# A decoder layer in one program: gathers moved behind low halves, transposes ahead of the first query, and another order at the end of cross attention

## The chip, the cores and the metric

The kernel runs on one core of a Trainium2 chip. The metric is the device time of one execution in microseconds (us). Five engines take part, each with its own instruction stream: TensorE (PE) multiplies, VectorE (DVE), ScalarE (ACT) and GpSimd (POOL) work elementwise, and SyncE (SP) issues DMAs. They wait for each other through semaphores that the kernel places by hand.

## The reference, cut to what matters

The input `x` is 32 sequences of 64 tokens of width 512, so 2048 rows. Three blocks follow one another, each added to its input and normalised:

```python
x = layernorm(x + self_attention(x))     # 32 heads of 128, 8 key heads; keys are 16 cache blocks of 32 rows, k_cache[block_idx], and sequence 0's own 64
x = layernorm(x + cross_attention(x, ctx))   # 32 heads, 8 key heads, keys and values from ctx (same shape as x)
z = x @ W.T + b                          # 512 to 512
m = (x @ A) @ B * p                      # 8 experts of rank 16, summed
gamma = minimum(0.5 * norm(z) / (norm(m) + eps), 1)
x = layernorm(x + z + gamma * m)
```

In self attention all 2048 rows see the same 576 keys. In cross attention each sequence sees its own 64.

## The kernel before, in words

Every float32 product is made of three products of a high and a low half: `a_hi b_hi + a_lo b_hi + a_hi b_lo`. ACT writes the high half (a rounded copy), DVE or POOL the low half (the difference). So each operand passes PE's bank, ACT, then DVE or POOL, before PE may use it.

**Phase one, self attention (`GROUPS` = 64 groups k).** A group is two heads for one half of the rows. Each has 8 score tiles `i` of 128 rows by 576 keys: PE `score(i)`, DVE `maximum(i)`, ACT `exponent(i)`, DVE `turn(i)` (a transpose in blocks), ACT `turned_hi(i)` (the high half, `pth`), POOL `low(i)` (the low half, `ptl`). The tile `8(k+1)` and up are made while group k is in `values(k)`, which waits for `low(8k+7)`. Then `project(k, t)`, t = 0 to 3, applies `wo`. `k = 4g + c`: four groups share one key head g. At c = 0, 1, 2 a small task prepares the next head's new keys, the turned keys and the new values. POOL also issues the indirect DMAs: `gather_k(g+2)` at c = 3 and `gather_v(g+1)` at c = 1, four each, from the cache blocks that `block_idx` names; ACT's `values_hi` and POOL's `values_low` split what was gathered.

**The start.** PE runs `query(0, 0)`, `turn_keys(0)`, and on through the first scores, with `query(1, 1)` behind `score(6)`. `query(0,0)` needs x tiles 0 to 3 and the first weight, in both halves. DVE's list of low halves and maxima is written by hand: `FIRST` are the loads (x tiles, `wq`, `wk`, `wv`).

**Phase two, cross attention (`STEPS` = 64 steps n).** A step is one head of 16 sequences: PE runs `score2(n)`, `values2(n-1)`, two blocks of the query of a later step, `project2(n-1, 0)` and `(n-1, 1)`, and keys and values of the next key head (`key2`, and `value_rows2` for odd heads). DVE sums and turns the scores, subtracts the maxima, inverts the sums and turns back. The layer norm of earlier tiles is spread over steps: `NORM_STEPS` and `NORM3_STEPS` say at which steps DVE and ACT normalise a pair of tiles. PSUM banks are handed round in an order that `bank_order` computes from the PE order, and `LAST_BANKS` names a few.

**The end.** In steps 60 to 63 the first eight tiles of x3 (the input of the last block) are turned by `turn_acc`, and split into `yTh`, `yTl`. `low_rank(q)` multiplies four tiles with A into `u`, `low_rank_out(tt)` with B, `linear(tt)` with W. Behind the last step each engine closes its semaphores and waits for all others (`"two"`), then phase three runs over 16 tiles `tt`: PE turns tile `tt+6`, does `linear(tt)` and `low_rank_out(tt)`; ACT takes norms (`norm_z`, `norm_m`, `norm_root`, `scaled_m`), DVE does `z_out` and `mix`, POOL `add_z` and `add_m`. `low_rank(q)` comes at `tt % 4 == 3`.

The lines that the rows below name: L1865 is `products` (all three-term sums), L1858 `turn_blocks`, L1937 `score`, L1957 `values`, L774 the indirect DMA in `gather`, L799 `low` on POOL, L534 and L571 the low halves of weights and the rotation, L954 ACT's high half of the gathered values, L529 ACT's high half of a load, L1457 `statistics`, L1690 the sum of scores, L1680 the swap of halves, L1412 `query_lo`, L1358 the low half of x tiles turned, L1540 `low_rank_lo`.

## Time and profile before

| | |
|---|---|
| time, median of 3 runs | 2743.34 us (2742.24 to 2744.5) |
| profiled execution, time | 2743.87 us |
| profiled execution, span | 2742.1 us |
| PE busy | 2684.1 us, 98% |
| DVE, POOL, ACT busy | 74%, 59%, 56% |
| mean granted clock of PE | 0.994 |

Phase one runs to about 1640 us, cross attention to about 2665, the last block to the end. How to read it: the busy share of an engine is an average over the span. "Idle before" in a timeline row is the time for which the engine stood still ahead of that instruction, and the arrow names the instruction that released it. The granted clock is 1.00 for 2.4 GHz and 0.50 for 1.2 GHz.

### The profile page before, as it was taken

The numbers are of one execution on the slowest core, as the hardware profiler recorded it, in microseconds if no ns is written. First come the engines' busy times: TensorE is split into PE (matmuls) and PEld (weight loads), VectorE is DVE, ScalarE is ACT, GpSimd is POOL, SyncE is SP. The second block draws the span as 40 slices with busy tenths as digits, with TensorE's granted clock in tenths as the row PEclk, the third lists the DMA queues.
The fourth block names the chain that finished last, engine by engine and source line by source line (L and its number), as shares of the span: only waits on it lengthen the run. The fifth ranks groups of instructions, "written<-read, shape, count | busy, mean of one in ns | idle before, by whom it ended". The sixth has DMA issues, their size and how long they took to land.

```text
span 2742.1 us, 64050 instructions
## 1 busy us (share of the span) xinstructions
PE 2684.1 (98%) x26496; PEld 2374.8 (87%) x26496; DVE 2022.1 (74%) x4005; ACT 1537.9 (56%) x3207; POOL 1621.1 (59%) x1379
## 2 busy tenths in 40 slices
PE   7999999999999999999999999999999999999997
PEld 6889888889899999999998988888888888888876
DVE  6676667667677777667777668887778878777887
ACT  5566566656666665666665645554445455444445
POOL 6887887788777666676666763232324433333235
PEclk9999999999999999999999999999999999999998
DMA  6233223323325313322331331111112111111111
GB/s 177 77 93 99 86 80 103 94 70 104 107 61 168 92 48 88 84 72 72 84 87 52 83 98 43 35 54 39 45 41 59 51 43 40 50 35 43 32 32 62
DMA packets 91483, 197.70 MB, mean 72 GB/s; under 512 B 20664, under 2 KB 21304, under 8 KB 89144
## 3 DMA queue, kind: packets, MB, share of 16 engines
q1 hardware_dynamic: 71480, 154.80, 20.2%
q10 hardware_dynamic: 17664, 34.61, 3.8%
q8 instruction: 209, 3.42, 0.5%
q0 software_dynamic: 2048, 4.20, 0.5%
q14 instruction: 82, 0.67, 0.1%
HBM read 176.78 MB, written 16.78 MB: 71 GB/s over the span
## 4 chain that ended last, share of the span: by engine, by line
PE 84%; POOL 7%; DVE 5%; issue 2%; ACT 1%; DMA 0%; DVEq 0%; ACTq 0%
PE bank L1865 29%; PE big L1865 28%; PE bank L1957 14%; PE big L1937 12%; POOL ptl L799 3%; POOL gathered L774 2%; PE big L1957 2%; POOL wqTl L534 1%; ACT pth L981 0%; DVE xol L1514 0%; DVE P L1690 0%; POOL wkvTl L534 0%; PE big L1858 0%; POOL oTl L804 0%; DVE nmx L1417 0%
## 5 line engine op out<-in xcount | busy, mean ns | idle before, releaser
L799 POOL TENSOR_TENSOR ptl<-P,pth 128x576 fp32r<-128x576 f32 x512 | 727.5, 1438 | 291.1 <-ACT pth L981 290.6
L972 ACT ACTIVATE P<-big,nmx 128x576 f32<-128x576 f32 x512 | 378.4, 739 | 345.8 <-DVE nmx L1417 313.5
L1423 DVE STREAM_TRANSPOSE P<-P 128x576 f32<-128x576 f32 x512 | 395.2, 772 | 152.6 <-ACT P L972 147.2
L1957 PE MATMUL bank<-pth,v 32*128 32x256 f32 x4608 | 426.9, 282 | 11.0 <-POOL ptl L799 8.2
L1417 DVE TENSOR_REDUCE nmx<-big 128x1 f32<-128x576 f32 x512 | 384.8, 753 | 71.3 <-PE big L1937 58.2
L1957 PE MATMUL big<-pth,v 32*128 32x256 f32 x4608 | 427.4, 282 | 0.5 <-issue 0.4
L1957 PEld LDWEIGHTS bank<-pth,v 32*128 32x128 f32 x4608 | 364.6, 188 | 22.3 <-POOL ptl L799 11.9
L1957 PEld LDWEIGHTS big<-pth,v 32*128 32x128 f32 x4608 | 369.4, 188 | 1.0 <-issue 1.0
L981 ACT ACTIVATE pth<-P 128x576 fp32r<-128x576 f32 x512 | 340.6, 678 | 39.7 <-DVE P L1423 39.4
L880 POOL TENSOR_TENSOR P<-P,sm 128x512 f32<-128x512 f32 x64 | 67.3, 1051 | 487.3 <-DVE sm L1719 487.3
L1957 PE MATMUL big<-ptl,v 32*128 32x256 f32 x2304 | 336.4, 279 | 0.0
L1957 PE MATMUL bank<-ptl,v 32*128 32x256 f32 x2304 | 331.0, 279 | 0.0
L1957 PEld LDWEIGHTS big<-ptl,v 32*128 32x128 f32 x2304 | 231.3, 188 | 0.0
L1937 PE MATMUL big<-kTh,qTh 128*128 128x288 f32 x1024 | 224.9, 301 | 6.6 <-ACT P L972 5.8
L804 POOL TENSOR_TENSOR oTl<-rall,oTh 128x256 fp32r<-128x256 f32 x256 | 183.5, 740 | 80.3 <-ACT oTh L987 80.3
L1957 PEld LDWEIGHTS bank<-ptl,v 32*128 32x128 f32 x2304 | 226.1, 188 | 0.0
L1937 PE MATMUL big<-kTl,qTh 128*128 128x288 f32 x1024 | 220.1, 296 | 0.0
L1937 PE MATMUL big<-kTh,qTl 128*128 128x288 f32 x1024 | 219.0, 295 | 0.0
L1937 PEld LDWEIGHTS big<-kTh,qTh 128*128 128x128 f32 x1024 | 180.5, 189 | 41.5 <-ACT P L972 6.1
L987 ACT ACTIVATE oTh<-rall 128x256 fp32r<-128x256 f32 x256 | 93.4, 412 | 187.4 <-DVE rall L1439 187.4
L1439 DVE TENSOR_TENSOR rall<-bank,rall 128x256 f32<-128x256 f32 x128 | 48.3, 419 | 200.8 <-PE big L1957 200.8
L534 POOL TENSOR_TENSOR wqTl<-raw,wqTh 128x512 fp32r<-128x512 f32 x126 | 162.1, 1298 | 7.2 <-ACT wqTh L529 6.9
(283 smaller groups left out, 8008.5 us busy)
## 6 DMA issues: line engine op xcount, KB each, us to landing
rall<-kept_r ACTq DMA_DIRECT2D x64, 512.0 KB
raw<-in_wo SPq DMA_DIRECT2D x64, 256.0 KB
raw<-in_xWq SPq DMA_DIRECT2D x64, 256.0 KB
raw<-in_xWo SPq DMA_DIRECT2D x64, 256.0 KB
raw<-in_wq SPq DMA_DIRECT2D x62, 256.0 KB
v<-kept_v SPq DMA_DIRECT2D x24, 448.0 KB
v<-kept_v SPq DMA_DIRECT2D x68, 128.0 KB, 3.0
raw<-in_xWkv SPq DMA_DIRECT2D x32, 256.0 KB
```

What stands on the lines that cost most here:

```text
L534: engine.tensor_tensor(lo, split_source(kind, n), f(hi), ALU.subtract).then_inc(signal((kind, n)), 1)
L799: pool.tensor_tensor(third_columns(ptl, i), blocks_of(i), f(third_columns(pth, i)), ALU.subtract).then_inc(p_low(i), 1)
L804: pool.tensor_tensor(out_quarter(ol[:, :, :], a), rall_quarter(a), f(out_quarter(oh[:, :, :], a)), ALU.subtract).then_inc(o_low((k, a)), 1)
L880: pool.tensor_tensor(pv, pv, sm2[:, :].unsqueeze(2).to_broadcast([128, 16, 32]), ALU.mult).then_inc(p_norm((2, n)), 1)
L972: act.activation(P[:, i % PSLOTS, :].rearrange("p (k n) -> p k n", k=2), ps_s[i % 2][:, :, 0:HALF], ACT.Exp, bias=nmx[:, i % 8:i % 8 + 1], ...
L981: act.activation(third_columns(pth, i), blocks_of(i), ACT.Copy).then_inc(p_hi(i), 1)
L987: act.activation(out_quarter(oh[:, :, :], a), rall_quarter(a), ACT.Copy).then_inc(o_hi((k, a)), 1)
L1417: dve.tensor_reduce(nmx[:, i % 8:i % 8 + 1], ps_s[i % 2][:, :, 0:HALF], AX.XY, ALU.max, negate=True).then_inc(max_done(i), 1)
L1423: dve.transpose(P[:, i % PSLOTS, :], P[:, i % PSLOTS, :]).then_inc(p_turned(i), 1)
L1865: t = pe.matmul(dst, a, b, start=first and i == 0, stop=final and end)
L1937: m = pe.matmul(ps_s[i % 2][:, h, 0:HALF], l, r[:, HALF * h:HALF * h + HALF], start=j == 0, stop=j == 2)
L1957: m = pe.matmul(ps_o[a][:, 0:256], v[r, s, l, :], p[r, lo:hi + 1:hi - lo, block_of(b), :, :], start=first, stop=final)
```

## The change: what it does

- **Gathers.** In groups `4g+1` POOL issues `gather_v(g+1)` behind `low(8(k+1)+6)` and `+7` and no longer behind `+5`.
- **Start.** PE makes 40 transposes of the identity into a score bank ahead of `query(0,0)`. The transposes' result isn't read. DVE takes three of the low halves of `FIRST` earlier (6, 7 ahead of the rotation, 8 ahead of the first maximum), `maximum(8)` ahead of `turn(7)` and `query_lo(1,1)` behind it; ACT takes `query_hi(1,1)` behind `exponent(7)`; PE takes `query(1,1)` ahead of `score(6)`.
- **Norms.** The last of the four norms in each half of cross attention moves from step 9 to 12 and from 41 to 44.
- **End.** The steps 62 and 63 are written out on PE, ACT and DVE in a new order. Tiles of x3 at steps 60 and 61 go to the banks of the values. `linear(0)` and `linear(1)` have banks of their own; `linear(2)`, `linear(3)`, `low_rank_out(0)` and `(1)` stand ahead of the last projection. `low_rank` 1, 2, 3 come at `tt` 1, 7, 11 (before: ahead of the last projection, 7, 11 on PE, 3, 7, 11 on ACT and DVE), and the odd ones go to another buffer (`low_rank_at`). ACT's norms and DVE's mixing of tiles 0 and 1, and POOL's `add_z` of both, stand ahead of the wait `"two"`.
- A few SBUF buffers stand in another order.

```diff
-NORM_STEPS = (5, 6, 7, 9)
-NORM3_STEPS = (37, 38, 39, 41)
+LOW_RANK_TILES = (1, 7, 11)
+NORM_STEPS = (5, 6, 7, 12)
+NORM3_STEPS = (37, 38, 39, 44)
...
-LAST_BANKS = [(("w", STEPS - 1, 0), 3), (("w", STEPS - 1, 1), 1)]
+LAST_BANKS = [(("u", 0), 0), (("w", STEPS - 3, 0), 1), (("w", STEPS - 3, 1), 3), (("x3", 4), 2), (("x3", 5), 0),
+              (("z", 0), 1), (("x3", 6), 3), (("x3", 7), 2), (("z", 1), 0), (("w", STEPS - 2, 0), 1),
+              (("w", STEPS - 2, 1), 3), (("w", STEPS - 1, 0), 0), (("w", STEPS - 1, 1), 1)]
...
+        def low_rank_at(q):
+            return (uTh, uTl) if q % 2 == 0 else (flat(q2h[:, 0]), flat(q2l[:, 0]))
...
-                if 0 <= g < G - 1 and c == 1:
-                    gather_v(g + 1)
...
+                if 0 <= g < G - 1 and c == 1:
+                    gather_v(g + 1)
...
+            add_z(0)
+            add_z(1)
...
-                if q >= 1:
-                    gate.wait_ge(ff_done, ("m", 4 * q - 1))
+                if q == 1:
+                    gate.wait_ge(s_done, (2, STEPS - 1, 1))
+                elif q >= 2:
+                    gate.wait_ge(ff_done, ("m", 4 * q - 5))
...
+            query_hi(1, 1)
+            exponent(8)
             turned_hi(7)
             keep_sums(0)
-            exponent(8)
             exponent(9)
             turned_hi(8)
             turned_hi(9)
-            query_hi(1, 1)
...
+            n = STEPS - 2
+            low_scores(n)
+            out2_hi(n - 1)
+            for a in blocks_at(n // 4, n % 4):
+                weight2(*a)
+            low_rank_hi(0)
+            exponential(n)
+            for tt in early_x3(n):
+                tile_high("x3", tt)
+            probability_hi(n)
+            n = STEPS - 1
+            low_scores(n)
+            out2_hi(n - 1)
+            for tt in early_x3(n):
+                tile_high("x3", tt)
+            exponential(n)
+            probability_hi(n)
+            out2_hi(n)
...
+            norm_z(0)
+            norm_m(0)
+            norm_root(0)
+            norm_z(1)
+            norm_m(1)
+            scaled_m(0)
+            norm_root(1)
+            scaled_m(1)
+            for s in (*of_pe, *of_dve, *of_pool, in_bob, in_pcol, *in_raw):
+                gate.wait_ge(s, "two")
...
+            weight_low(*FIRST[6])
+            weight_low(*FIRST[7])
             rotate(dve, gate, prep, 0)
             query_lo(0, 0)
             key_lo(0)
             new_key_lo(0, ps_o[1])
-            weight_low(*FIRST[6])
-            weight_low(*FIRST[7])
+            weight_low(*FIRST[8])
...
+            maximum(8)
             turn(7)
+            query_lo(1, 1)
             invert_sums(0)
-            maximum(8)
             maximum(9)
             turn(8)
             turn(9)
-            query_lo(1, 1)
...
+            n = STEPS - 2
+            sum_scores(n)
+            out2_lo(n - 1)
+            turn_scores(n)
+            maxima(n)
+            low_rank_lo(0)
+            half_sums(n)
+            add_out2(n - 1, 0)
+            invert_sums2(n)
+            turn_back(n)
+            add_out2(n - 1, 1)
+            for tt in early_x3(n):
+                tile_low("x3", tt)
+            z_out(0)
+            n = STEPS - 1
+            sum_scores(n)
+            out2_lo(n - 1)
+            tile_low("x3", early_x3(n)[0])
+            turn_scores(n)
+            maxima(n)
+            tile_low("x3", early_x3(n)[1])
+            half_sums(n)
+            invert_sums2(n)
+            z_out(1)
+            turn_back(n)
+            add_out2(n - 1, 0)
+            add_out2(n - 1, 1)
+            statistics(pairs2(GG - 1, 0), 2)
+            statistics(pairs2(GG - 1, 1), 2)
+            out2_lo(n)
...
+            add_out2(STEPS - 1, 0)
+            for tt in range(2):
+                for step in range(4):
+                    mix(tt, step + 1)
+                z_out(tt + 2)
+            add_out2(STEPS - 1, 1)
+            for s in (*of_dve, acc_done, ln):
+                s.close("two")
+            for s in (*of_pe, *of_act, *of_pool, in_bob, in_pcol, *in_raw):
+                gate.wait_ge(s, "two")
...
+            gate.wait_ge(pool_init, "ident")
+            for i in range(40):
+                pe.transpose(ps_s[0][:, 0, 0:128], ident[:, :], ident[:, :])
...
-            score(6)
             query(1, 1)
-            for i in range(7, 12):
+            for i in range(6, 12):
...
+            n = STEPS - 2
+            score2(n)
+            values2(n - 1)
+            low_rank(0)
+            project2(n - 1, 0)
+            project2(n - 1, 1)
+            for tt in early_x3(n):
+                turn_acc("x3", tt)
+            linear(0)
+            n = STEPS - 1
+            score2(n)
+            for tt in early_x3(n):
+                turn_acc("x3", tt)
+            values2(n - 1)
+            linear(1)
+            project2(n - 1, 0)
+            project2(n - 1, 1)
+            low_rank(1)
+            linear(2)
+            values2(n)
+            linear(3)
+            project2(n, 0)
+            wait_over(0)
+            low_rank_out(0)
+            wait_over(1)
+            low_rank_out(1)
+            project2(n, 1)
+            ring[0] = 0
...
-                if tt % 4 == 3 and 2 <= tt // 4 + 1 < 4:
-                    low_rank(tt // 4 + 1)
+                if tt in LOW_RANK_TILES[1:]:
+                    low_rank(LOW_RANK_TILES.index(tt) + 1)
                 if tt >= NT - 2:
                     low_rank_out(tt)
-                if tt >= 2:
+                if tt >= 4:
                     linear(tt)
-                if tt < NT - 2:
+                if 2 <= tt < NT - 2:
```

## Rows read from the trace of the kernel before

**Rows 1.** The page, busy time of each engine
```profile
PE 2684.1 (98%) x26496; PEld 2374.8 (87%) x26496; DVE 2022.1 (74%) x4005; ACT 1537.9 (56%) x3207; POOL 1621.1 (59%) x1379
```

**Rows 2.** Waits of PE, whole span: us in total, times, longest
```profile
PE bank L1957 <- POOL ptl L799: 8.2, 7, 2.9
```

**Rows 3.** Timeline of PE, starts of values: start, us, operation, idle before
```profile
74.28 0.38 PE L1957 MATMUL bank<-pth,v 32*128 32x256 f32 x2
...
103.04 0.58 PE L1957 MATMUL bank<-pth,v 32*128 32x256 f32 x2 [2.88 <-POOL ptl L799]
...
179.28 0.38 PE L1957 MATMUL bank<-pth,v 32*128 32x256 f32 x2
...
204.93 0.38 PE L1957 MATMUL bank<-pth,v 32*128 32x256 f32 x2 [0.91 <-POOL ptl L799]
...
757.04 0.38 PE L1957 MATMUL bank<-pth,v 32*128 32x256 f32 x2
...
781.24 0.38 PE L1957 MATMUL bank<-pth,v 32*128 32x256 f32 x2
```

**Rows 4.** Windows: PE, PEld, DVE, ACT, POOL busy; clock, DMA share, GB/s
```profile
103.00:106.00 3.00, 2.96 (x56) 2.96 (x60) 1.15 (x2) 2.63 (x6) 3.00 (x3) 0.50 0.03 5
```

**Rows 5.** Timeline of POOL in group 5, gathers and low halves
```profile
194.82 0.98 POOL L774 DMA_INDIRECT gathered<-in_v_cache,idx  x1
...
202.09 5.58 POOL L799 TENSOR_TENSOR ptl<-P,pth 128x576 fp32r<-128x576 f32 x4
```

**Rows 6.** Windows of the cross-attention steps 9, 10 and 11
```profile
1781.85:1796.26 14.41, 14.41 (x83) 12.24 (x81) 12.60 (x29) 7.81 (x15) 6.26 (x6) 1.00 0.24 73
1796.26:1811.53 15.27, 14.84 (x82) 12.07 (x81) 12.54 (x34) 8.16 (x14) 3.49 (x3) 1.00 0.12 35
1811.53:1826.97 15.44, 14.54 (x82) 12.24 (x81) 12.93 (x31) 8.50 (x17) 7.47 (x7) 1.00 0.16 53
```

**Rows 7.** Timeline of DVE: the norm behind step 9, and score sums
```profile
1797.49 1.28 DVE L1457 BATCH_NORM_STATS2 stat<-xaccb 128x6 f32<-128x512 f32 x2
...
1800.65 1.41 DVE L1690 TENSOR_TENSOR P<-big,P 64x512 f32<-64x512 f32 x2
...
1845.57 1.41 DVE L1690 TENSOR_TENSOR P<-big,P 64x512 f32<-64x512 f32 x2 [2.29 <-ACT P L1202]
```

**Rows 8.** Timeline of PE at the start
```profile
8.95 0.76 PE L1865 MATMUL bank<-xTh,wqTh 128*128 128x512 f32 x1 [8.95 <-issue]
...
14.95 0.63 PE L1858 MATMUL big<-ident,gathered 128*128 128x128 f32 x4 [0.74 <-DVE gathered L571]
...
27.01 0.50 PE L1865 MATMUL bank<-xTh,wqTh 128*128 128x512 f32 x1 [1.06 <-DVE xTl L534]
...
46.66 0.58 PE L1957 MATMUL bank<-pth,v 32*128 32x256 f32 x2 [1.49 <-DVE qTl L1412]
```

**Rows 9.** Timeline of ACT behind the start
```profile
53.50 0.63 ACT L529 ACTIVATE wqTh<-raw 128x512 fp32r<-128x512 f32 x1 [3.90 <-DMA raw<-in_wq]
```

**Rows 10.** Windows, from step 61 to PE's last instruction
```profile
2600.00:2727.50 127.50, 119.69 (x576) 96.58 (x574) 104.52 (x264) 66.05 (x158) 58.11 (x46) 0.97 0.11 38
```

**Rows 11.** Timelines of PE, DVE and POOL at the end
```profile
2679.31 0.51 PE L1865 MATMUL big<-wkvTh,uTh 128*128 128x512 f32 x1 [1.99 <-DVE uTl L1540]
...
2673.96 0.60 PE L1858 MATMUL big<-ident,xaccb 128*128 128x128 f32 x4
...
2671.87 0.69 DVE L1358 TENSOR_TENSOR yTl<-big,yTh 128x512 fp32r<-128x512 f32 x1 [2.06 <-ACT yTh L920]
...
2630.02 2.19 DVE L1680 TENSOR_TENSOR mxo<-mx 32x16 f32<-32x16 f32 x4
...
2629.24 2.54 POOL L534 TENSOR_TENSOR xTl<-raw,xTh 128x512 fp32r<-128x512 f32 x2 [1.27 <-ACT xTh L529]
```

**Rows 12.** The chain of waits at the start; timeline of ACT in group 5
```profile
7.44 4.99 DMA gathered<-in_k_cache,idx
...
217.88 0.62 ACT L954 ACTIVATE gathered<-gathered 128x512 fp32r<-128x512 f32 x1
```

More of the change, by code:

```diff
@@ L1192, in scalar_program, with low_scores @@
             value2_hi(0, 2)
-            for n in range(STEPS):
-                g, s = n // 4, n % 4
-                work = blocks_at(g, s)
-                last = n == STEPS - 1
+            rows2 = flat(P2[:, :, :])
+            def low_scores(n):
                 for par in range(2):
@@ L1280, in scaled_m, with shift_tile @@
                     ff_hi(("gm", tt)), 1)
+            for s in (*of_act, root):
+                s.close("two")
+            norm_z(0)
[8 more added lines that the diff above has]
+                gate.wait_ge(s, "two")
+            def shift_tile(tt):
+                gate.wait_ge(ln, ("shift", 3, tt))
+                act.activation(xa(tt), xa(tt), ACT.Identity, bias=mv[:, tt, 0:1], scale=rstd[:, tt:tt + 1]).then_inc(
+                    ff_hi(("norm", tt)), 1)
             for tt in range(NT):
@@ L1321, in put @@
                 turn += 1
-            for n in range(STEPS):
+            for n in range(STEPS - 2):
                 g, s = n // 4, n % 4
@@ L1336, in bank_order @@
                     put(("w", n - 1, 1))
-                if n < STEPS - 2:
-                    for tt in early_x3(n):
-                        put(("x3", tt))
                 if n == 0:
```

239 lines of the change are left out of this document (103 added, 136 removed).

## The prediction

> **What bounds the kernel now.** I read the page's engine table first: TensorE (PE) is busy 98% of a span of 2742.1 us, VectorE (DVE) 74%, the others less [rows 1]. So PE's instruction stream sets the end, and an edit is worth only what it takes from PE's idle time, from PE's time at the lower clock, or from the tail behind PE's last matmul. Second, the waits of PE over the whole span: the largest entry is PE waiting in `values` for the low half of the probabilities from GpSimd (POOL), 8.2 us in seven waits, the longest 2.9 [rows 2]. Third, the timeline of PE at the starts of `values(k)`: the reader should compare intervals. Two neighbours with nothing extra lie 24.20 apart (757.04 to 781.24); 179.28 to 204.93, where keys are also turned, is 25.65 and ends in an idle 0.91 on POOL; 74.28 to 103.04 is 28.76 and ends in an idle 2.88 [rows 3]. Behind that last wait PE runs 3 us at a granted clock of 0.50, 1.2 GHz of 2.4, after an idle stretch [rows 4]. The other losses of PE sit at two steps of cross attention, in the first 47 us, and behind 2600 us; each is read below.
>
> **Gathers behind low halves.** In group k = 4g+1 POOL issues four indirect DMAs for the values of the next key head between the low half of tile 5 and those of tiles 6 and 7 of the next row. They occupy it from 194.82 to about 199.5, then come two weight low halves, and only at 202.09 the run of `low`s whose second one `values(6)` waits for at 204.93 [rows 3, 5]. Four issues at 0.95 plus three pauses of 0.3 are 4.7 us, and PE waits 0.9: with the gathers behind the two `low`s these end some 4 us before PE asks, and the whole stall goes. It occurs six times at 0.9 (8.2 less the 2.9) = 5.4. The first time costs more: 28.76 against 25.65 less 0.91 is 4.0, and three microseconds at half clock give back 1.5. Sum 10.9. At most 11.4 (if a restart of PE costs 0.1 more each time), at least the idle time alone, 8.2. What is now late: the gathers move past `low(8(k+1)+6)` and `+7` and stand ahead of `low(8(k+2))`, `+1`, which are delayed by no more than before since POOL's work ahead of them is the same. ACT's exponents of the next row wait for those two; they are asked for about 6 us later, by my reading of the same timeline. The similar gather of keys in groups 4g+3 stays.
>
> **Norms from steps 9 and 41 to 12 and 44.** A step of cross attention with an even head takes 14.41; the two behind step 9's norm take 15.27 and 15.44 [rows 6]: 0.86 + 1.03 = 1.9, and the same again at 41, so 3.8. The block holds DVE from 1797.49 to 1800.65, 3.16 us [rows 7]. Steps 12 and 44 have an odd head and more matmuls (`value_rows2`). There DVE sits idle 2.29 before its next score sum [rows 7], so the block makes that sum 0.87 late, where before a block of 3.16 cost a step 0.86 and 1.03 with no such idle time ahead of it. I take the 0.87 as hidden; if all of it reached PE, twice, 2.0 of 3.8 is left.
>
> **The start.** `query(0,0)` begins at 8.95, when DVE's low half of the inputs is there, and ends at 14.21; the turn of the keys then waits 0.74 for DVE's rotation, which hangs on the gather of keys [rows 8]. Forty transposes ahead of it end before 8.95 (four take 0.60 at most [rows 11], forty 6.0, from about 1.5), so they cost nothing, and a faster first query gains nothing, because its end is not what is late. The DVE order counts: x tile 5's low half moves ahead of the first maximum, so the wait of 1.06 at 27.01 goes; `query_lo(1,1)` moves up on DVE and ACT, so the wait of 1.49 at 46.66 goes [rows 8]: 2.6. The two low halves moved ahead of the rotation fit into the time in which DVE waits for the gather (the chain of waits has that DMA to 12.43 [rows 12]). `score(6)` goes behind `query(1,1)`, hidden as DVE reaches its maximum only later. The interval 46.66 to 74.28 is 27.62 [rows 3, 8], 2.0 over the 25.65 of a later one, which I lay to the lower clock behind idle PE; I take a third of it back, 0.6. Sum 3.2. The next bound is ACT, which waits 3.90 for a weight load at 53.50 and holds the exponent that `score(13)` needs [rows 9]; that chain also moves, but by about 2.6. Bounds: -1 (the scores before `values(0)` now leave PE idle in more pieces and may run at the lower clock) and +5.
>
> **The end.** From 2600 to PE's end at 2727.5 PE is busy 119.69 of 127.5 and its clock is 0.97 [rows 10]: 7.8 idle and 3.8 of clock, 11.6 to be had at most. The new order puts tiles of x3 into the banks of the values, starts `linear(0)` in step 62 instead of 63, does `linear(2)`, `linear(3)` and two `low_rank_out` ahead of the last projection, computes the second low-rank tile into its own buffer, and puts ACT's and DVE's norms of tiles 0 and 1 ahead of the wait common to all engines. The work is the same; it fills the holes of steps 62 and 63. By my walk through those steps with the durations of before PE reaches the last projection at about the same time as now but with 6.8 us more done (two times 2.73 and 0.68). This can't be kept whole: DVE gets to the low half of tile 8 at 2671.87 now, after waiting 2.06 [rows 11]; in the new order it has the norms of tiles 0 and 1, two z sums and the low half of u ahead of it, and I put it at 2671.2. PE needs it for its turn of tile 10, at 2673.96 now [rows 11]: 2.7 gained. The wait of 1.99 for u at 2679.31 [rows 11] goes (u has been ready for 8 us), and with it a fall of the clock like the one of rows 4, 1.5. Sum 6.2; bounds 2.0 (only the wait for u) and 11.6. From there DVE has 3.6 us of work for a tile of 3.9 on PE, estimated from the same timeline, so it follows.
>
> One row speaks for less. At 2630.02 four copies of 32 partitions take DVE 2.19 us, ending with POOL's weight low halves that began at 2629.24 [rows 11]. The Trainium skill (SBUF — State Buffer, "Who interferes with whom") says that a DVE instruction with two SBUF inputs and a GpSimd instruction that reads SBUF block each other for a whole instruction. By that rule the move of `add_z(0)`, `add_z(1)` to beside DVE's norms adds up to two such waits. The trace agrees, and at 1.3 a wait (the POOL row shows 2.54 for two) the end would give 3.6 instead of 6.2, which is within the bounds above.
>
> **Sum.** 10.9 + 3.8 + 3.2 + 6.2 = 24.1. The profiled execution took 2743.87, 1.8 more than its span and 0.5 more than the median 2743.34; 2743.9 - 24.1 = 2719.8, and on the scale of the median 2719.3. I say 2719.
>
> **Rivals.**
> A. DVE is the bound of the end: it is busy 104.5 of 127.5 there [rows 10], and taking PE's holes away only makes PE wait for DVE later. For it: DVE's share; against: it waits 2.06 at tile 8. The end gives nothing: 2725.5.
> B. The stall moves from POOL to ACT: the `low`s of the last two tiles are themselves held by ACT's high halves, so gathers out of the way gain nothing. Against it: the four `low`s from 202.09 run without a pause, 5.58 for four [rows 5], so POOL was the late one. 2743.4 - 13.2 = 2730.
> C. The transposes pay by themselves. The first query takes 5.3 for twelve matmuls, where the 576 matmuls and transposes behind 2600 take 0.21 each, 2.5 for twelve [rows 10]; if the query's end were what is late, 2.8 more would come. Against it: the 0.74 of rows 8. 2716.5. The Trainium skill (TensorE: Matmul & The Clock Gate, "What's actually happening") says the array starts throttled and activity releases it, by which the forty transposes would let the first query run at 2.4 GHz; the rows at 8.95 and 27.01 (0.76 and 0.50 for a first matmul) agree that the start is slow.
> D. Slower: the gather lands too late for ACT. ACT's high half of the gathered values at 217.88 stands in front of its exponents [rows 12]. The gathers now end their issue near 205.5, and the one that the trace shows lands 5.0 after its issue began [rows 12], so 6 us are to spare. If landing took more than 11.5, ACT would wait, and PE behind it, seven times; from 15 us on it eats the 24 us of gain. At 20 it would be 60 - 24 lost: 2779.
> E. The changes hide behind each other and nothing moves: 2743.
>
> **Chances.** Forecast 0.75, A 0.11, B 0.05, C 0.03, D 0.03, E 0.03. The range takes in A and most of the bounds: lows of the four parts together would give 2731, highs 2711; 2712 to 2729 should hold 8 times in 10. About 0.2% (5.5 us) can be told from no change: faster by more 0.94, within 0.03, slower 0.03.
>
> **What would show it.** In the trace after: no wait of PE on POOL in `values` at k = 4g+2, and the intervals of `values` there near 24.7; steps 10, 11, 42, 43 at 14.41, and 13, 45 at 17.3; `values(0)` near 44; turns of x3 tiles with no wait on u; PE's clock above 0.97 behind 2600. Wrong, if PE waits for ACT's exponents behind the gathered values, if steps 13 or 45 grow, or if DVE is busy without a pause from 2640 on while PE waits.

## The result, and the profile after

| | before | after |
|---|---|---|
| time, median of 4 runs | 2742.79 us (2740.95 to 2744.5) | 2727.61 us (2726.09 to 2728.54) |
| profiled execution, time and span | 2743.87, 2742.1 | 2728.54, 2726.7 |
| mean granted clock of PE | 0.994 | 0.992 |

The ratio is 0.9941, with a 95% interval of 0.9929 to 0.9953: the kernel is 15.2 us faster by the medians. I had said 2719, 24 us faster, with a range of 2712 to 2729. So the direction and the range held, the range by 1.4 us, and 9 of the 24 us did not come. The page of the changed kernel, part 1, stands against [rows 1]: PE has hardly more to do (40 transposes), and its idle time is less.

```profile
PE 2687.8 (99%) x26536; PEld 2381.6 (87%) x26536; DVE 2022.2 (74%) x4005; ACT 1539.0 (56%) x3207; POOL 1621.5 (59%) x1379
```

In the rows of the changed kernel the lines have other numbers: L1934 is `products`, L1927 `turn_blocks`, L2006 `score`, L2026 `values`, L780 the indirect DMA, L805 `low` on POOL, L535 and L540 the halves of a load, L570 to L577 the rotation, L962 ACT's high half of the gathered values, L1475 DVE's addition of a projection, L1388 the low half of x tiles turned, L1571 `low_rank_lo`, L1487 to L1501 a layer norm on DVE, L899 and L911 POOL's `add_z` and `add_m`.

The waits of PE in the changed kernel (us in total, times, longest). The entry of [rows 2], 8.2 us on POOL in `values`, is gone. Of the longest entries two were small or absent before, and both belong to parts that I had credited with a gain: the wait for DVE's `yTl` at the end, and that for the rotation (`gathered`) at the start.

```profile
PE big L1927 <- DVE yTl L1388: 4.6, 1, 4.6
...
PE big L1927 <- DVE gathered L577: 3.1, 1, 3.1
PE bank L2026 <- DVE xacc L1475: 2.0, 8, 0.6
```

Where the 15.3 us between the two traces lie is read from the starts of the same work in both, each from the timeline of PE. `score2(n)` is the first work of step n:

| start of | before | after | gained so far | gained in this stretch |
|---|---|---|---|---|
| `values(0)` | 46.66 | 46.75 | -0.1 | start: -0.1 |
| `values(1)` | 74.28 | 73.90 | 0.4 | 0.5 |
| `values(29)` | 781.24 | 772.03 | 9.2 | gathers: 8.8 |
| `values(63)` | 1602.33 | 1594.34 | 8.0 | -1.2 |
| `score2(60)` | 2593.97 | 2582.30 | 11.7 | norms: 3.7 |
| PE's last matmul | 2727.09 | 2711.75 | 15.3 | end: 3.7 |

The tail behind the last matmul is 15.0 us in both. The gathers gave 8.8 of 10.9, the norms 3.7 of 3.8, the end 3.7 of 6.2, the start nearly nothing of 3.2, and a place that I had not looked at took 1.2 back. This is one trace against one; the experiments below show which of these sizes return in other traces.

**Gathers.** Timelines of PE (the starts of `values(2)` and `values(6)`), POOL and ACT of the changed kernel; they answer to [rows 3, 5, 12].

```profile
98.84 0.38 PE L2026 MATMUL bank<-pth,v 32*128 32x256 f32 x2 [0.21 <-DVE xacc L1475]
...
198.74 0.39 PE L2026 MATMUL bank<-pth,v 32*128 32x256 f32 x2 [0.19 <-DVE xacc L1475]
...
193.88 1.43 POOL L805 TENSOR_TENSOR ptl<-P,pth 128x576 fp32r<-128x576 f32 x1 [0.79 <-ACT pth L989]
195.46 0.98 POOL L780 DMA_INDIRECT gathered<-in_v_cache,idx  x1 [0.15 <-issue]
...
200.22 2.83 POOL L805 TENSOR_TENSOR ptl<-P,pth 128x576 fp32r<-128x576 f32 x2
...
211.69 0.62 ACT L962 ACTIVATE gathered<-gathered 128x512 fp32r<-128x512 f32 x1
```

The low half that `values(6)` needs ends at 195.3, 3.4 us before the start, and the gathers follow it. PE no longer waits for POOL, but it waits 0.2 for DVE, which adds the last projection to the residual. So the interval went from 25.64 to 24.95, not to 24.74. ACT takes its high half of the gathered values at 211.69 with no idle time ahead of it.

**Norms.** Windows of steps 9 to 12 of cross attention (columns as in [rows 4]), against [rows 6].

```profile
1773.94:1788.36 14.42, 14.42 (x83) 12.25 (x81) 12.60 (x29) 7.83 (x15) 6.27 (x6) 1.00 0.26 74
1788.36:1802.77 14.41, 14.41 (x82) 12.24 (x81) 11.48 (x28) 7.33 (x14) 5.35 (x5) 1.00 0.12 36
1802.77:1817.18 14.41, 14.41 (x82) 12.24 (x81) 11.47 (x28) 6.81 (x13) 6.12 (x6) 1.00 0.22 56
1817.18:1834.48 17.30, 17.30 (x107) 15.13 (x105) 14.34 (x33) 9.08 (x16) 7.30 (x6) 1.00 0.15 46
```

Steps 10 and 11 are back at 14.41 with PE busy all the time, and so is step 12 at 17.30; steps 13 and 45 take 17.29 too. The block is free where it now stands.

### The profile page after: what moved, and what is told of

It reads as the page before. It is cut to its first block, busy times and chain, and to the rows that moved or that the text cites. A ratio compares the mean times of both kernels' runs of the same rounds, so it can differ in the third digit from the quotient of the medians.

```text
span 2726.7 us, 64132 instructions
## 1 busy us (share of the span) xinstructions
PE 2687.8 (99%) x26536; PEld 2381.6 (87%) x26536; DVE 2022.2 (74%) x4005; ACT 1539.0 (56%) x3207; POOL 1621.5 (59%) x1379
## 4 chain that ended last, share of the span: by engine, by line
PE 91%; DVE 4%; POOL 3%; ACT 1%; issue 1%; DMA 0%; SPq 0%; ACTq 0%; DVEq 0%
PE bank L1934 30%; PE big L1934 30%; PE bank L2026 14%; PE big L2006 14%; PE big L2026 2%; POOL ptl L805 1%; POOL gathered L780 1%; PE big L1927 0%; DVE P L1453 0%; DVE nmx L1447 0%; POOL wqTl L540 0%; DMA xacc<-in_xt 0%; ACT P L980 0%; DVE xacc L1475 0%; DVE xol L1544 0%
## 5 line engine op out<-in xcount | busy, mean ns | idle before, releaser
L805 POOL TENSOR_TENSOR ptl<-P,pth 128x576 fp32r<-128x576 f32 x512 | 728.2, 1437 | 295.3 <-ACT pth L989 294.7
L2026 PE MATMUL bank<-pth,v 32*128 32x256 f32 x4608 | 425.2, 281 | 2.9 <-DVE xacc L1475 2.0
L2026 PE MATMUL big<-pth,v 32*128 32x256 f32 x4608 | 425.3, 281 | 0.0
L2026 PEld LDWEIGHTS bank<-pth,v 32*128 32x128 f32 x4608 | 365.9, 187 | 14.1 <-issue 11.8
L2026 PEld LDWEIGHTS big<-pth,v 32*128 32x128 f32 x4608 | 367.4, 187 | 0.0
L2026 PE MATMUL big<-ptl,v 32*128 32x256 f32 x2304 | 334.9, 278 | 0.0
L2026 PE MATMUL bank<-ptl,v 32*128 32x256 f32 x2304 | 332.8, 278 | 0.0
L2006 PE MATMUL big<-kTh,qTh 128*128 128x288 f32 x1024 | 225.7, 302 | 5.2 <-ACT P L980 4.4
L2026 PEld LDWEIGHTS big<-ptl,v 32*128 32x128 f32 x2304 | 230.2, 187 | 0.2 <-issue 0.2
L2026 PEld LDWEIGHTS bank<-ptl,v 32*128 32x128 f32 x2304 | 228.1, 187 | 0.0
L2006 PE MATMUL big<-kTl,qTh 128*128 128x288 f32 x1024 | 220.9, 297 | 0.0
L2006 PE MATMUL big<-kTh,qTl 128*128 128x288 f32 x1024 | 219.6, 296 | 0.0
L2006 PEld LDWEIGHTS big<-kTh,qTh 128*128 128x128 f32 x1024 | 181.2, 189 | 40.1 <-ACT P L980 3.5
L2006 PEld LDWEIGHTS big<-kTh,qTl 128*128 128x128 f32 x1024 | 166.4, 190 | 0.0
```

The lines of the kernel that those rows point to most:

```text
L805: pool.tensor_tensor(third_columns(ptl, i), blocks_of(i), f(third_columns(pth, i)), ALU.subtract).then_inc(p_low(i), 1)
L2006: m = pe.matmul(ps_s[i % 2][:, h, 0:HALF], l, r[:, HALF * h:HALF * h + HALF], start=j == 0, stop=j == 2)
L2026: m = pe.matmul(ps_o[a][:, 0:256], v[r, s, l, :], p[r, lo:hi + 1:hi - lo, block_of(b), :, :], start=first, stop=final)
```

## The experiments

### The gathers alone

```diff
 # kernel before
-                if 0 <= g < G - 1 and c == 1:
-                    gather_v(g + 1)
...
                     low(8 * (k + 1) + 7)
+                if 0 <= g < G - 1 and c == 1:
+                    gather_v(g + 1)
```

> The kernel before with the gathers of values behind the two low halves and nothing else. Theory of the prediction (POOL issues four gathers while PE needs the low half): the idle of PE before the values of groups 4g+2 goes from 0.9 to what DVE leaves, about 0.2, the seven intervals from 25.65 to 24.95 and the first from 28.76 to about 25, its follower from 26.3 to 25.0: 9.3 us less at the start of values 29 (781.2 to 771.9), and 2734 us for the whole. Rival (the stall moves to ACT's high halves): the intervals stay at 25.6 and the time within 2 us of the kernel before. Rival (gathered values land too late): ACT waits ahead of the high half of the gathered values, and PE in groups 4g+3; slower than before.

Measured: 2733.23 us (6 runs, 2732.09 to 2733.96), ratio 0.9964 (0.9951 to 0.9976), 10 us faster. `values(29)` starts at 770.36, 10.9 earlier than before; but 2.5 of that is there at `values(1)` already (71.82 against 74.28), ahead of the first moved gather, in a start that has the same instructions. The part that the gathers can have made is 8.4. The six intervals at groups 4g+1 behind the first are 24.94 or 24.95, as in the changed kernel. The first is 25.65, where the changed kernel has 24.94 and 25 was expected: PE waited 0.46 more for the low half `oTl` on its way. Of the thirteen traces with the moved gathers seven have 24.94 there, one 25.09 and five 25.6 to 25.8, so this first interval is not a fixed number. ACT's wait did not come, so the theory stands and both rivals fall.

This run also showed that two traces of the same start can differ by 2.5 us, and that the interval from `values(62)` to `values(63)` was 23.02, as in the changed kernel, against 21.85 before: the 1.2 us lost there are not the work of any edit near it.

### The start, four ways, and the rotation ahead of two low halves

```diff
 # no_transposes and no_transposes_again: changed kernel
-            gate.wait_ge(pool_init, "ident")
-            for i in range(40):
-                pe.transpose(ps_s[0][:, 0, 0:128], ident[:, :], ident[:, :])
 # rotation_first: changed kernel
-            weight_low(*FIRST[6])
-            weight_low(*FIRST[7])
             rotate(dve, gate, prep, 0)
             query_lo(0, 0)
             key_lo(0)
             new_key_lo(0, ps_o[1])
+            weight_low(*FIRST[6])
+            weight_low(*FIRST[7])
 # start_old: changed kernel, but all of PE, DVE and ACT up to score 11 as before
 # start_old_transposes: start_old, with the 40 transposes
 # change_again: the changed kernel
```

> The changed kernel without the 40 transposes ahead of the first query. Theory 1 (the transposes only lengthen PE's idle behind the query, since the rotation of the keys is what is late, and the longer idle brings the clock down for longer): the first query runs at half clock again, 5.2 us instead of 2.8, the idle before the keys' turn is under 1 us instead of 3.1, the first score starts no later than 20.0 and values(0) starts 0 to 1.5 us earlier than 46.75. Theory 2 (the transposes bring what they are meant to and another edit eats it): values(0) starts 1 to 2.5 us later than 46.75, the whole takes 2729 to 2730.

> The changed kernel with DVE's low halves of the second weight and of x tile 4 back behind the rotation of the keys. Theory (these two wait for their loads, to 11.6 and 12.9, and hold the rotation back from 12.45 to 13.52): the rotation starts near 12.5, the keys' turn about 1 us earlier than 15.92, values(0) starts near 45.7 instead of 46.75, the whole takes about 1 us less. Rival (they fit into DVE's wait for the gather, and the later start in the changed kernel comes from loads of x that land later): the rotation starts at 13.5 again and values(0) at 46.7.

> The changed kernel itself, on the chip of the next three, so that the four make a square: with or without the 40 transposes, new or old order of the start. Expected 2726 to 2728.

> The changed kernel without the 40 transposes, once more and in more rounds. Theory (the transposes lengthen PE's idle and bring the clock down for longer): 1 to 2.5 us less than the changed kernel. Rival (the one look was luck, the transposes change nothing at the end of the start): within 0.7 us of it.

> The changed kernel with the whole start of before: no transposes, and the old order of PE, DVE and ACT up to score 11. The prediction gave the new start 3.2 us. Theory from the traces (the new start as a whole brings nothing or costs 1 us): this takes 0 to 1.5 us less than the changed kernel. Rival (the prediction's term): it takes 2 to 4 us more.

> The changed kernel with the old order of the start but with the 40 transposes. Theory (the rotation is not held back by low halves here, so the first query's 2.8 us again only lengthen the wait for it, to some 2 us): within 1 us of start_old, or up to 2 us more through the clock. Rival (the transposes pay when the order leaves them room): 1 to 2.5 us less than start_old.

Measured, with the start of `values(2)` in each trace (the first point behind the start; in the kernel before it would be at 99.2, that is 103.04 less the 3.8 that the gathers gave there):

| kernel | median us (runs) | lowest to highest | `values(2)` |
|---|---|---|---|
| change_again | 2725.17 (5) | 2723.71 to 2728.45 | 97.18 |
| no_transposes_again | 2727.24 (5) | 2725.52 to 2728.63 | 99.19 |
| start_old | 2727.08 (5) | 2724.77 to 2728.34 | 97.54 |
| start_old_transposes | 2727.51 (5) | 2724.25 to 2731.49 | 102.80 |
| no_transposes | 2725.95 (4) | 2724.98 to 2731.13 | 97.22 |
| rotation_first | 2728.43 (4) | 2725.23 to 2729.82 | 95.55 |

The first four ran on one chip. Their ratios to the kernel before are 0.9939, 0.9941, 0.9940 and 0.9940, each with an interval of about 3.6 us either way: the start as a whole, its transposes and its order are each worth nothing that these runs can tell. By the medians no_transposes_again is 2.1 us above change_again, which neither its theory nor its rival had, and start_old 1.9, just short of its rival's 2 to 4; the ranges overlap. The nine executions of the changed kernel (both sets) have a mean of 2726.6, the five of start_old 2726.7, and the difference is known to about 2 us; so a start worth 3.2 us is hardly left, one worth 1 us is. The traces say the same: `values(2)` comes at 99.2, 97.47 (gathers_only) and 97.54 with the old start, 98.1 on average, and at 96.74 to 100.74, 98.4 on average, in the five traces with the new one. The 2.5 us by which `values(0)` came earlier in no_transposes (44.28 against 46.75) were luck: the repetition gave 46.77 there, and the changed kernel's own repetition 45.25. The theory that the transposes cost 1 to 2.5 us fell in that repetition, and the prediction's 3.2 us fell as well.

rotation_first bore out its theory in the trace, where the rotation started at 11.55 and `values(0)` at 43.56, and not in the time: 2728.43 with a ratio of 0.9949, where 1 us less was expected. Its trace is of the fastest of its four executions; the others took 2728.07 to 2729.82.

What the traces do show is a mechanism on either side. Timelines of PE and DVE of the changed kernel, then PE of start_old:

```profile
9.85 0.47 PE L1934 MATMUL bank<-xTh,wqTh 128*128 128x512 f32 x1 [1.58 <-DVE xTl L540]
15.92 0.87 PE L1927 MATMUL big<-ident,gathered 128*128 128x128 f32 x4 [3.10 <-DVE gathered L577]
...
11.59 0.69 DVE L540 TENSOR_TENSOR wqTl<-xacc,wqTh 128x512 fp32r<-128x512 f32 x1 [0.62 <-ACT wqTh L535]
12.91 0.69 DVE L540 TENSOR_TENSOR xTl<-xacc,xTh 128x512 fp32r<-128x512 f32 x1 [0.63 <-ACT xTh L535]
13.52 0.75 DVE L570 TENSOR_TENSOR gathered<-gathered,turns 128x256 f32<-128x256 f32 x2
```

```profile
10.01 0.76 PE L1934 MATMUL bank<-xTh,wqTh 128*128 128x512 f32 x1 [10.01 <-DVE xTl L540]
14.26 0.60 PE L1927 MATMUL big<-ident,gathered 128*128 128x128 f32 x4
```

With the transposes the first query takes 2.97 us (from 9.85 to the turn's 15.92 less its wait), without them 4.25 in start_old and 5.26 before. So it is faster, as rival C said, but the keys' turn waits for DVE's rotation, and PE now stands still for 3.10 us. DVE in turn waits 0.62 and 0.63 for ACT's halves of loads that have just landed, and only then starts the rotation: the two low halves did not fit into its wait for the gather. In start_old the turn follows with no wait. When the gather lands differs from trace to trace, as the rotation shows where nothing else stands ahead of it; timelines of DVE in rotation_first and start_old_transposes:

```profile
11.55 0.76 DVE L570 TENSOR_TENSOR gathered<-gathered,turns 128x256 f32<-128x256 f32 x2 [1.28 <-DMA gathered<-in_k_cache,idx]
```

```profile
13.66 0.76 DVE L570 TENSOR_TENSOR gathered<-gathered,turns 128x256 f32<-128x256 f32 x2 [3.01 <-DMA gathered<-in_k_cache,idx]
```

Windows of 17 to 20 and 20 to 23 us of the changed kernel, then of start_old (columns as in [rows 4]):

```profile
17.00:20.00 3.00, 2.19 (x12) 2.08 (x11) 1.12 (x3) 1.20 (x4) 2.09 (x4) 0.50 0.14 44
20.00:23.00 3.00, 3.00 (x12) 3.00 (x13) 1.21 (x2) 1.48 (x4) 2.98 (x3) 0.50 0.18 49
```

```profile
17.00:20.00 3.00, 3.00 (x19) 2.74 (x20) 2.84 (x5) 2.23 (x5) 2.67 (x3) 1.00 0.18 45
20.00:23.00 3.00, 3.00 (x26) 2.77 (x25) 2.60 (x4) 2.81 (x6) 1.40 (x2) 1.00 0.00 0
```

start_old_transposes, where no low half stands ahead of the rotation, had the same wait in its trace, 3.54 us, and the same slow clock behind it, and the latest `values(2)` of all; but its gather landed last too, so this trace alone doesn't charge the transposes. The rival, that the transposes pay when the order leaves them room, has no support in its time either.

Behind the 3.10 us the clock is 0.50 for some 7 us, and what the faster query brings is spent. There is a second such place, ahead of `values(0)`. Windows of the changed kernel, then of start_old:

```profile
40.20:50.30 10.10, 8.61 (x82) 7.94 (x86) 6.48 (x11) 6.92 (x15) 5.50 (x5) 0.50 0.63 146
```

```profile
40.50:47.20 6.70, 5.87 (x60) 5.55 (x64) 4.30 (x6) 5.12 (x12) 0.92 (x2) 0.50 0.28 74
47.30:50.30 3.00, 3.00 (x109) 3.00 (x108) 0.00 (x0) 0.23 (x1) 3.00 (x3) 1.00 0.59 157
```

All fourteen traces have these places, and they give a rough split:

| | traces | PE's wait ahead of the turn | first score starts |
|---|---|---|---|
| 40 transposes, no filling behind the query | 7 | 1.83 to 3.98 | 16.69 to 20.40, mean 19.1 |
| no transposes | 5 | 0 to 1.42 | 16.93 to 18.07, mean 17.6 |

From the first score to `values(2)` the new order takes 78.7 to 81.1 us (eight traces without filling, 79.4 on average), the old order with the moved gathers 80.1 to 82.4 (three, 81.0), although the slow stretch ahead of `values(0)` lasts 10.2 us in five of those eight and 6.8 in every trace of the old order. So the new order of the scores is worth some 1.7 us, the transposes go with a first score some 1.5 us later, and the two cancel. The ranges overlap, and the low halves of x alone are ready up to 1.5 us apart from trace to trace (the first query started between 8.7 and 10.2), so these are sizes and not proofs.

### The clock: transposes in PE's waits

```diff
 # start_fill: rotation_first, and
             query(0, 0)
+            for i in range(10):
+                pe.transpose(ps_s[0][:, 0, 0:128], ident[:, :], ident[:, :])
             turn_keys(0)
...
             for i in range(6, 12):
+                if i >= 9:
+                    ps = out_place(1, None)
+                    for j in range({9: 9, 10: 6, 11: 3}[i]):
+                        pe.transpose(ps[:, 0:128], ident[:, :], ident[:, :])
                 score(i)
 # group_fill: changed kernel, in project(k, t)
                 ps = out_place(out_bank(k, t), (acc_done, (k, t)))
+                if k == GROUPS - 2 and t == 0:
+                    for i in range(9):
+                        pe.transpose(ps[:, 0:128], ident[:, :], ident[:, :])
 # end_fill: changed kernel, ahead of turn_acc("x3", 10)
+                if tt == 4:
+                    gate.wait_ge(ff_lo, ("z", 2))
+                    for i in range(24):
+                        pe.transpose(ps_z[0][:, 0:128], ident[:, :], ident[:, :])
```

> The changed kernel with 9 transposes of the identity into the output bank of the first projection of group 62, in PE's wait of 1.89 us there. Theory (behind this wait the clock falls, for 1.7 us before and for 5 us after the change, which took back 1.2 us of the gain): the interval from values 62 to values 63, 23.02 to 23.07 in four kernels and 21.84 in two, is 20.5 to 21.3. Rival (the interval is set by what the wait waits for, and its spread by chance of another kind): 21.8 to 23.1 again.

> The changed kernel with 24 transposes of the identity into an idle bank ahead of the turn of tile 10, where PE waited 4.64 us; their result is not read. Theory (the idle itself costs what DVE's lateness costs and nothing that PE does can change it, but the slow clock behind it is a second price): the wait shrinks to about 0.6 and the turn starts at the same distance from the last score sum, but the matmuls behind it start 0.23 apart and not 0.43, some 1.5 to 2 us less at PE's last matmul. Rival (the clock behind a wait is not the wait's doing): the matmuls behind the turn stay 0.43 apart for some 3 us, and the time is that of the changed kernel.

> rotation_first, and transposes of the identity in PE's waits of the start as well: 10 between the first query and the keys' turn, 9, 6 and 3 ahead of scores 9, 10 and 11. Theory (with the waits filled the clock stays at its high level from the first query on): first score near 16.7, the scores 1 to 8 1.5 to 2 us earlier, values(0) near 42.5 unless the loads of kept values hold it (it waited 1.36 for one at 44.28 without the transposes), and the interval to values(1) about 25 instead of 27.05; values(2) starts 2 to 4 us earlier than 95.55. Rival (the start is bound by DVE, ACT and loads): values(2) within 1 us of 95.55.

**group_fill**: 2725.02 us (4 runs, 2723.32 to 2727.71), within the spread of the changed kernel. The interval from `values(62)` to `values(63)` is 20.25, a little below the 20.5 to 21.3 expected. PE's timeline and a window of the changed kernel, then of group_fill:

```profile
1583.66 0.76 PE L1934 MATMUL bank<-woTh,oTh 128*128 128x512 f32 x1 [1.89 <-issue]
...
1585.00:1587.00 2.00, 2.00 (x7) 1.62 (x6) 0.13 (x1) 0.68 (x1) 2.00 (x2) 0.50 0.00 0
```

```profile
1583.49 1.15 PE L2036 MATMUL bank<-ident 128*128 128x128 f32 x9
1585.51 0.50 PE L1934 MATMUL bank<-woTh,oTh 128*128 128x512 f32 x1 [0.87 <-POOL oTl L810]
...
1583.00:1586.00 3.00, 2.13 (x16) 1.85 (x16) 2.10 (x3) 2.73 (x6) 3.00 (x5) 1.00 0.00 0
```

The wait is filed under "issue" in the one and under POOL's low half in the other, where the rest of it is 0.87; behind it the clock stays at 1.00. The fourteen traces have this interval in three groups: 21.6 to 21.9 in seven, 22.9 to 23.1 in five, and 20.25 and 20.30 in the two with the filling. The granted clock tells the groups apart: behind this wait it is 0.50 for 3.4 us in the seven, for 6.8 us in the five, and never in the two. Windows of the changed kernel (23.07), then of change_again (21.85):

```profile
1583.00:1589.70 6.70, 6.04 (x17) 5.10 (x18) 2.59 (x5) 3.35 (x7) 5.91 (x5) 0.50 0.15 39
```

```profile
1582.50:1585.70 3.20, 3.20 (x12) 2.82 (x11) 0.78 (x1) 1.23 (x3) 3.20 (x3) 0.50 0.00 0
1586.00:1589.70 3.70, 3.70 (x18) 3.04 (x17) 3.37 (x7) 1.52 (x3) 1.83 (x2) 1.00 0.24 71
```

The kernel before and the changed one, each profiled once, fell into different groups, and that is the 1.2 us of the table. change_again is the same code as the changed kernel. So this loss belongs to the profiled execution and not to the change.

**end_fill**: 2726.10 us (4 runs, 2725.25 to 2727.72), within the spread of the changed kernel; the trace resolves it. Timeline of PE and a window of the changed kernel, then of end_fill:

```profile
2660.72 1.12 PE L1927 MATMUL big<-ident,xaccb 128*128 128x128 f32 x4 [4.64 <-DVE yTl L1388]
...
2661.00:2664.00 3.00, 3.00 (x10) 2.52 (x10) 2.83 (x10) 1.84 (x6) 1.07 (x1) 0.50 0.02 5
```

```profile
2655.01 2.78 PE L2360 MATMUL big<-ident 128*128 128x128 f32 x24
2659.86 0.66 PE L1927 MATMUL big<-ident,xaccb 128*128 128x128 f32 x4 [2.06 <-DVE yTl L1388]
...
2661.00:2664.00 3.00, 3.00 (x15) 2.40 (x15) 2.26 (x7) 2.08 (x6) 1.95 (x2) 1.00 0.00 0
```

From the turn to PE's last matmul it is 49.1 us with the filling and 51.0 without: 1.9 us for the clock alone. The nine traces with the 4.64 us wait take 50.5 to 51.9 there. The transposes took 0.12 us each here, so 24 of them filled 2.8 us and not the 4 that I had meant, and 2.06 of waiting was left; that did not bring the clock down.

**start_fill**: 2723.90 us (4 runs, 2722.66 to 2724.59). Its ratio is 0.9931 (0.9915 to 0.9948), and it is 3.7 us below the changed kernel and 1.3 below change_again. The clock from 36 to 42 us is 1.00 where rotation_first had 0.56, `values(2)` starts at 94.49, 1.1 earlier than rotation_first and 2.3 to 6.3 earlier than in the five traces of the unchanged new start. The interval to `values(1)` is 27.05 again and not 25: the clock fell for 3.4 us just behind the start of `values(0)`, whose matmuls are 0.21 apart from 43.4 to 46.1 and 0.12 behind that. I had expected `values(2)` 2 to 4 us earlier than in rotation_first; 1.1 is hardly more than the 1 us of the rival. A part of the slow clock has another place than the waits that I filled, and rotation_first's trace was itself an early one.

### The norm of the last two tiles, later

```diff
 # changed kernel, ACT and DVE
-                if tt == 0:
+                if tt == 2:
                     square_root([NT - 2, NT - 1], 2)
...
-                if tt == 0:
+                if tt == 2:
                     normal3([NT - 2, NT - 1])
```

> The changed kernel with the layer norm of tiles 14 and 15 (DVE statistics and normalise, ACT's root) moved from tile step 0 to tile step 2 of the last block, behind the low half of tile 8. Theory (PE's 4.64 us wait ahead of the turn of tile 10 is DVE's and ACT's norm of tiles 14 and 15, 4.5 us, standing ahead of tile 8): the wait falls to under 1.5 us and the clock stays up, 3 to 5 us less, 2722.6 to 2724.6. Rival A of the prediction (DVE is the bound of the end, work moved behind one tile is paid at the next): the wait shows up again at the turns of tiles 11 to 13 and the whole gains less than 1.5 us.

Measured: 2723.91 us (4 runs, 2722.30 to 2725.08), 3.7 less than the changed kernel's 2727.61 and 1.3 less than change_again's 2725.17; the ratio is 0.9929 (0.9912 to 0.9945) against their 0.9941 and 0.9939. The time alone doesn't settle the size; the trace does. Timeline of DVE in the changed kernel: what stands between the last score work and tile 8's low half.

```profile
2654.80 1.29 DVE L1487 BATCH_NORM_STATS2 stat<-xaccb 128x6 f32<-128x512 f32 x2
...
2658.03 1.38 DVE L1501 TENSOR_SCALAR xaccb<-xaccb,mv,rstd 128x512 f32<-128x512 f32 x2
2659.33 0.74 DVE L1571 SCALAR_TENSOR_TENSOR xql<-bank,pcol,xqh 128x512 fp32r<-128x512 f32 x1
2659.99 1.49 DVE L1388 TENSOR_TENSOR yTl<-big,yTh 128x512 fp32r<-128x512 f32 x2
```

And with the norm later, DVE and then PE:

```profile
2655.45 0.75 DVE L1571 SCALAR_TENSOR_TENSOR xql<-bank,pcol,xqh 128x512 fp32r<-128x512 f32 x1 [0.78 <-PE big L1927]
2656.12 0.68 DVE L1388 TENSOR_TENSOR yTl<-big,yTh 128x512 fp32r<-128x512 f32 x1
2656.72 1.28 DVE L1487 BATCH_NORM_STATS2 stat<-xaccb 128x6 f32<-128x512 f32 x2
...
2656.86 0.66 PE L1927 MATMUL big<-ident,xaccb 128*128 128x128 f32 x4 [0.78 <-DVE yTl L1388]
2680.57 0.50 PE L1934 MATMUL bank<-wkvTh,uTh 128*128 128x512 f32 x1 [1.42 <-DVE uTl L1571]
```

The wait falls from 4.64 to 0.78, and PE's last matmul comes at 2708.30 instead of 2711.75, 3.45 earlier, with `score2(63)` at the same time in both (2625.30, 2625.27). 3.86 of wait and the slow clock went, 1.42 came back as a wait for u, and the rest is spent in small pieces. Rival A, DVE as the bound of the end, would have given the whole 3.86 back at the next tiles; of those 3.86 and the 1.9 of clock 2.3 were given back, less than half.

### All together

> start_fill, group_fill and last_norm_later in one. Theory (the three losses lie apart and add): 3 to 6 us from the start against the changed kernel, 2 from group 63, 3.4 from the end, so 2716 to 2719 us. Rival (they hide behind each other): 2722 to 2725.

The edits of start_fill, group_fill and last_norm_later in one kernel: 2718.12 us (4 runs, 2717.48 to 2719.20), ratio to the kernel before 0.9911 (0.9894 to 0.9927). The changed kernel's two medians were 2727.61 and 2725.17, so this is 7 to 9.5 us less, within the 2716 to 2719 expected. In the trace `values(2)` comes at 94.48, the interval behind `values(62)` is 20.30, and from `score2(60)` to the last matmul it takes 126.6: against the averages of the unfilled traces some 4, 2 and 3 us. The losses lie apart and add, as expected. It is the fastest of the kernels here.

## Why the prediction came out 8.6 us too low

**What held.** The direction, and one of the four parts at its size. The norms to 0.1 us: DVE's idle time ahead of the next score sum took the 3.16 us block. The gathers' mechanism: POOL alone was late, the `low`s ran as soon as ACT had delivered, and the gathered values were in time. Rivals B, D and E fell with gathers_only. That the time lies in the range is in part luck: 2727.61 is 1.4 us below its upper end and nearer to rival A's 2725.5 than to 2719, though A's mechanism, an end that gives nothing, isn't what happened. The lows of the four parts also add up to 2732 and not to the 2731 of the prediction.

**Gathers: the term was mis-sized, 10.9 for a measured 8.4 to 8.8.** The first occurrence was 5.5 in the sum and 5.1 in the trace of after (28.76 to 24.94, and 26.30 to 25.00 at the slow clock behind it), and 4.4 in gathers_only (25.65 and 25.01). The six others were put at the full idle time, 0.9. They gave 0.69 each, 4.1 and not 5.4, since DVE's addition is late by 0.2 once POOL isn't. I had written that the whole stall goes and had named only POOL and ACT as what is late next. Against these sums, 9.3 and 8.5, the trace of after lost 0.4 in one interval (25.40 for 25.00) and gathers_only 0.1 in another.

**The start: the step that failed.** It rested on two waits of PE and on a sentence that the two low halves fit into DVE's wait for the gather. The waits at 27.01 and 46.66 did go [rows 8] (0.20 is left of the second), but they were points of a chain that loads, DVE and the clock set together. The second was mostly this one trace's: with the same old order it is 0.30 in gathers_only and 0.31 in start_old, so some 1.2 of the 3.2 belonged to that execution and not to the order. The two low halves need loads that come no sooner than the gather: in the changed kernel the rotation starts at 13.52, straight behind them, in rotation_first at 11.55. The 40 transposes were costed at nothing because they end before 8.95, which they did (6.74 us from 1.53); what I left out is that a query that takes 2.3 us less leaves PE idle for 3.1, and that the clock falls behind such a wait, the very thing that I had charged to the gathers. I had given rival C 0.03 as a gain; the Trainium skill (TensorE: Matmul & The Clock Gate, "What's actually happening") has the array throttled at the start until activity releases it, and the trace agrees: 0.47 for the first matmul of the query behind the transposes, 0.76 without. So that query is faster, and no time of the kernel comes of it. What the runs show lies between my lower bound of -1 and some 1 us. The reason that I gave for that bound came true as well: ahead of `values(0)` the clock is low for longer, 10.2 us for 6.8. That the whole start is worth less than 3.2 us is shown by the kernels above; how its gains and losses split is read from averages of traces whose ranges overlap.

**The end: the right gain, and half of it lost in two steps.** From `score2(60)` to the last matmul the nine traces with the unchanged new end take 128.7 to 131.6, 129.7 on average; the two with the old end 133.1 and 132.2. That is 2.9, and 3.7 in the pair of traces shown, for 6.2 predicted. I had put tile 8's low half on DVE at 2671.2 on the scale of before, and PE's turn of tile 10 with it. It began at 2659.99 in the trace of after, or 2671.7 with the 11.7 us that lie ahead, and PE's turn came 0.7 later, when the instruction was done: 2672.4, which is 1.6 earlier than before and not 2.7. So 0.5 is DVE's list and 0.7 the duration of the instruction itself, which I had left out. Nor did the list name the norm of tiles 14 and 15, which stands ahead of tile 8 in both kernels and is the part that can be moved. That norm took 4.5 us, where the same one took 3.2 before: two of its instructions ran beside POOL and were 1.3 us longer (rows below). Without these 1.3 us DVE would have been 0.8 ahead of my 2671.2. Second, I had counted 1.5 for a fall of the clock that goes with the wait for u [rows 11]. The wait for u did go, but the 4.64 us wait for tile 8 brought the clock down in its place; end_fill prices that at 1.9. Putting the norm behind tile 8 gave 3.4 more, and with it the end takes 126.1 and 126.6 us, 6.3 less than the old one. That this equals the 6.2 predicted is luck in its size, since it needed an edit that the prediction didn't have.

The feared collision of DVE and POOL came, at another place than I had looked. The Trainium skill (SBUF — State Buffer, "Who interferes with whom") has a two-input DVE instruction and a GpSimd instruction that reads SBUF block each other. The instructions that were held up here read one tensor each, so their rows are no test of that sentence. Beside POOL's two `add_z` a small one took 0.63 where its like took 0.17, and nothing waited for it. Beside POOL's `add_m` the same instruction of the last norm took 1.06 and ended with POOL's, and the normalising behind it 1.38 where it takes 1.00 alone; both stand ahead of tile 8's low half, for which PE waited. Timelines of POOL and DVE in the changed kernel, then of DVE in the kernel before, where POOL was idle there:

```profile
2641.33 2.54 POOL L899 TENSOR_TENSOR xacc<-xacc,z 128x512 f32<-128x512 f32 x2
2642.02 0.63 DVE L1492 TENSOR_SCALAR mv<-mv 128x2 f32<-128x2 f32 x1
2644.15 0.17 DVE L1492 TENSOR_SCALAR mv<-mv 128x2 f32<-128x2 f32 x1
...
2654.94 2.51 POOL L911 TENSOR_TENSOR xacc<-xacc,gm_m 128x512 f32<-128x512 f32 x2 [11.07 <-PE bank L1934]
2656.41 1.06 DVE L1492 TENSOR_SCALAR mv<-mv 128x2 f32<-128x2 f32 x1
```

```profile
2667.52 0.17 DVE L1462 TENSOR_SCALAR mv<-mv 128x2 f32<-128x2 f32 x1
```

The prediction had worked out 3.6 for the end with two such waits. The 3.7 of the pair of traces is near it by luck: one wait of that size came, and the slow clock behind tile 8's wait, which was in no term, cost 1.9.

**The last projections of phase one were in no step.** The profile of before had PE idle 1.91 behind `values(62)`, behind which a window of the same trace shows a clock of 0.57. I had read PE's waits by their releaser; this one is filed under "issue". The interval around it moves by 1.2 us from one execution to the next without any edit.

## What to carry to other kernels

A wait that is removed has to be followed by the question what is late next on each engine that feeds the same instruction, and only the distance to that one is gained: 0.7 of 0.9 here, and the last 4.5 us norm ahead of a tile is easily left out of such a list. A wait that a single trace shows in the start is checked in a second trace before it is counted: 1.49 here was 0.3 elsewhere. Making PE faster ahead of a point that something else sets lengthens its idle time there, and behind such a wait (1.8 to 4.0 us here) the clock was halved for 3.4 to 10.2 us; so count idle stretches of PE, not only their sum. Where such a wait can't be removed, dummy transposes in a free bank kept the clock up and paid 1.9 us at one place and 1.6 to 2.8 at another, as read in the traces; each alone stays within the spread of the times, and only all_fixed is clear of it. Ahead of the first query, where the next wait followed at once, they brought nothing.

## What the runs showed of the hardware

Behind the same 1.9 us wait of PE, with the same work around it, the clock was 0.50 for 3.4 us or for 6.8 us, and the interval from `values(62)` to `values(63)` 21.6 to 21.9 or 22.9 to 23.1 us. It fell in all twelve traces in which that wait was not filled, and behind the 4.64 us wait in all nine that have it. With transposes ahead of it a rest of 2.06 us left the clock at 1.00 in end_fill, and one of 0.87 in group_fill. In the start, traces of the same start code differ by up to 4 us at `values(2)` (96.74 and 100.74, end_fill and group_fill, which differ only far behind it). So a difference of a few us between two profiled executions of this kernel says nothing unless it is read at a place where the work is the same and the clock is full.

A 128x2 instruction on DVE took 0.17 us alone, and 0.63 and 1.06 beside POOL's additions of 128x512, the second until POOL's ended.
